# Scoring order of a token pass: the narrowest block's steps among a wide block's, another block at the end, and the passes without a loop

## The reference, cut to what matters

```python
x = x + _L0_conv_ref(_gn(x), L0_conv_W)                # sums of |w - patch|
x = _L1_conv_ref(x, ...)                               # two quantised 3x3 convolutions
t = _to_tokens(x)                                      # 16 images, 784 tokens, 128 channels
t = t + _L2_attn_ref(_ln_t(t), L2_attn_W, L2_attn_v)
t = t + _L2_ffn_ref(_ln_t(t), ...)                     # top 2 of 8 experts
t = t + _L3_attn_ref(_ln_t(t), ...)                    # causal linear attention
t = t + _L3_ffn_ref(_ln_t(t), ...)                     # spectral filters, plus 3 taps

def _L2_attn_ref(B, W, v):
    Wi = jnp.einsum('bnd,ed->bne', B, W)
    scores = jnp.einsum('d,bijd->bij', v, jnp.tanh(Wi[:, None, :, :] + Wi[:, :, None, :]))
    attn = jax.nn.softmax(scores, axis=-1)
    return jnp.einsum('bij,bjd->bid', attn, B)
```

## Time and profile before

| | |
|---|---|
| median of 3 runs (lowest, highest) | 12419.64 us (12418.51, 12423.34) |
| the profiled execution | 12419.25 us, span 12417.5 us |
| granted TensorE clock, mean of the span | 0.982 |
| first scoring matmul of pass 0; start of pass 2; last corner matmul | 6201.7, 6879.2, 12071.8 us |

### The profile page before, as it was taken

The page is one execution under the profiler, slowest core; times in us unless marked ns, Lnnn a source line. Parts: engine busy times, 40 slices in busy tenths (PEclk is TensorE's granted clock), DMA queues, the critical chain, the costliest instruction groups (busy, mean ns, idle before and its releaser), DMA issues. The chain is left out here.

```text
span 12417.5 us, 297675 instructions
## 1 busy us (share of the span) xinstructions
PE 11680.7 (94%) x123040; PEld 5800.0 (47%) x123040; DVE 11221.2 (90%) x20963; ACT 10972.2 (88%) x8020; POOL 125.0 (1%) x103
## 2 busy tenths in 40 slices
PE   8999999999999999999867999999999999999999
PEld 3333333333333333333323555555555555555567
DVE  9999999999999999999898888898888888888881
ACT  8999999999999999999788888888888888888872
POOL 0000000000000000000000000000000000000000
PEclk9999999999999999999988999999999999999999
DMA  0000000000000000000010111111111111111123
GB/s 14 2 7 2 3 6 2 7 2 4 4 2 7 2 4 4 2 4 2 16 51 3 45 53 53 53 54 50 50 53 53 54 54 50 52 51 55 51 57 109
DMA packets 290050, 355.16 MB, mean 29 GB/s; under 512 B 28040, under 2 KB 242960, under 8 KB 288656
## 3 DMA queue, kind: packets, MB, share of 16 engines
q1 hardware_dynamic: 288656, 335.48, 9.3%
HBM read 314.14 MB, written 21.23 MB: 27 GB/s over the span
## 5 line engine op out<-in xcount | busy, mean ns | idle before, releaser
L276 ACT ACTIVATE c_ring<-c_xn,c_w_neg 128x1568 f32<-128x1568 f32 x3824 | 5792.1, 1606 | 279.6 <-PE c_acc L235 273.0
L235 PE MATMUL c_acc<-c_ring,c_onehot 128*32 128x392 f32 x68608 | 5763.0, 493 | 138.5 <-DVE c_ring L434 78.8
L426 DVE TENSOR_SCALAR c_ring<-c_xn,c_w 128x1568 f32<-128x1568 f32 x4752 | 4572.9, 1036 | 93.2 <-PE c_acc L235 93.1
L1429 DVE TENSOR_SCALAR t_ring<-t_proj 128x172 f32<-128x172 f32 (+8 forms) x9664 | 3738.2, 462 | 361.4 <-PE t_psS L1010 330.7
L235 PEld LDWEIGHTS c_acc<-c_ring,c_onehot 128*32 128x32 f32 x68608 | 2217.4, 110 | 3658.0 <-issue 3209.2
L1110 ACT ACTIVATE t_ring<-t_ring 128x2624 f32<-128x2624 f32 (+63 forms) x1584 | 3306.5, 2118 | 502.8 <-DVE t_ring L1429 452.8
L1010 PE MATMUL t_psS<-t_ring,t_vhot 128*32 128x272 f32 (+22 forms) x36864 | 2369.8, 406 | 379.6 <-ACT t_ring L1109 165.9
L1010 PEld LDWEIGHTS t_psS<-t_ring,t_vhot 128*32 128x32 f32 x36864 | 1026.7, 113 | 1597.1 <-issue 918.9
L967 PE MATMUL t_psC<-t_filter_work 128*128 128x392 f32 (+3 forms) x6144 | 1654.4, 405 | 0.0
L967 PEld LDWEIGHTS t_psC<-t_filter_work 128*128 128x128 f32 x6144 | 1098.8, 190 | 688.0 <-issue 173.8
L434 DVE SCALAR_TENSOR_TENSOR c_ring<-c_xn,c_w,c_ring 128x784 f32<-128x784 f32 x1280 | 1267.6, 1034 | 95.8 <-ACT c_ring L276 94.8
(11 more groups left out here) (233 smaller groups left out, 3504.0 us busy)
## 6 DMA issues: line engine op xcount, KB each, us to landing
t_filter_work<-in_toep_dram SPq DMA_DIRECT2D x256, 393.0 KB, 3.4
t_filter_work<-mix_scratch SPq DMA_DIRECT2D x512, 192.0 KB, 2.5
t_filter_work<-in_toep_dram SPq DMA_DIRECT2D x256, 197.0 KB, 3.0
t_filter_work<-mix_scratch SPq DMA_DIRECT2D x512, 64.0 KB, 1.9
mix_scratch<-t_filter_work SPq DMA_DIRECT2D x4, 2048.0 KB, 9.5
c_xin<-in_x_dram SPq DMA_DIRECT2D x8, 784.0 KB, 4.3
x_scratch<-c_x1o SPq DMA_DIRECT2D x8, 784.0 KB, 3.4
t_proj<-x_scratch SPq DMA_DIRECT2D x16, 392.0 KB, 3.9
```

The source lines that it names most:

```text
L235: mm = pe.matmul(acc[32 * g:32 * g + 32, ch, 0:HALF], onehot[:, 31 - r:63 - r], ring[:, s % RING, g, ch * HALF:(ch + 1) * HALF], start=(s ...
L276: ins = act.activation(tile4(ring[:, s % RING, g, :]), window(xn, tap), ACT.Relu, bias=w0_neg[:, tap, 4 * r + g:4 * r + g + 1])
L426: dve.tensor_scalar(tile4(ring[:, s % RING, g, :]), window(xn, tap), w0[:, tap, 4 * r + g:4 * r + g + 1], 0.0, ALU.subtract, ALU.max).then ...
L1429: ins = dve.tensor_scalar(ring[:, st % RINGS, o + q * w:o + (q + 1) * w], proj[:, 128 * blk + first:T], proj[:, i:i + 1], None, ALU.add)
```

## The change

Block 5's steps are put among block 1's: one after every fourth, seven in all, and the corner after the last. Blocks then go 0, 4, 1 (with 5 and the corner), 2, 3, and block 3, two rows a step, ends the pass; its scores are copied out in the next. Batches follow the ends of blocks: after slot 86 (block 1's last) a batch comes one slot early and every fourth from there. Convolutions leave out batch 16; the last four mixes go together into batch 33, after the last slot. Side work past slot 86 moves by one slot or one batch, the next image's by one batch. Block 5's and the corner's matmuls no longer carry the flag that starts a sum, since block 1's first matmul has set their half bank. SyncE loads the next image when ScalarE, not VectorE, has ended the pass before. All passes are written out. No instruction that computes is added or taken away.

```diff
-ORDER = [0, 4, 1, 3, 2, 5, 6]
+ORDER = [0, 4, 1, 5, 6, 2, 3]
...
-START = {blk: sum(STEPS[o] for o in ORDER[:POS[blk]]) for blk in ORDER}
-NS = START[6]
+SLOTS = []
+for _blk in (0, 4, 1, 2, 3):
+    for _k in range(STEPS[_blk]):
+        SLOTS.append((_blk, _k))
+        if _blk == 1 and _k % 4 == 3 and _k // 4 < STEPS[5]: SLOTS.append((5, _k // 4))
+NS = len(SLOTS)
+END = {blk: 1 + max(st for st, slot in enumerate(SLOTS) if slot[0] == blk) for blk in STEPS}
...
-SLOTS = [(blk, k) for blk in ORDER[:6] for k in range(STEPS[blk])]
-assert len(SLOTS) == NS and NS % RINGS == 0
+assert sorted(SLOTS) == [(blk, k) for blk in range(6) for k in range(STEPS[blk])] and NS % RINGS == 0
...
-BATCHES = {min(GROUP * B + GROUP - 1, NS - 1) for B in range((NS + GROUP - 1) // GROUP)}
+BATCH_AT = [4 * B + 3 if 4 * B + 3 < END[1] else 4 * B + 2 for B in range((NS + GROUP - 1) // GROUP)]
+assert BATCH_AT[-1] == NS - 1 and all(END[blk] - 1 in BATCH_AT for blk in range(5))
 def batch(B, rank):
-    return min(GROUP * B + GROUP - 1, NS - 1) + rank
+    return BATCH_AT[B] + rank
+def filters_in(j):
+    return j if j < 16 else j + 1
...
+AT_LN = [dict(stats=28, aggr=30, norm=32, turn=batch(8, EARLY), evac=35), dict(stats=80, aggr=82, norm=84, turn=batch(21, EARLY), evac=86),
+         dict(stats=119, aggr=120, norm=122, turn=batch(31, EARLY), evac=126)]
...
-AT_STU = dict(u=batch(32, EARLY), uev=131, res=batch(3, LATE), resev=16, conv=[batch(u // 2, (FIRST, SECOND)[u % 2]) for u in range(64)], conved=[4 * (u // 2) + (3, 5)[u % 2] for u in range(64)],
-              mix=[batch(1 + m // 2, MIX) for m in range(64)], ar=[batch(1, EARLY), batch(17, EARLY)], out=[68, 1])
...
+AT_STU = dict(u=batch(32, EARLY), uev=130, res=batch(3, LATE), resev=16, conv=[batch(filters_in(u // 2), (FIRST, SECOND)[u % 2]) for u in range(64)],
+              conved=[int(batch(filters_in(u // 2), (0, 2)[u % 2])) for u in range(64)],
+              mix=[batch(1 + filters_in(min(m // 2, 29)) if m // 2 < 30 else 33, MIX) for m in range(64)], ar=[batch(1, EARLY), batch(17, EARLY)], out=[68, 1])
+AT_NEXT = dict(x=[batch(25, EARLY), batch(25, LATE)], tok=[102, 103], ln=dict(stats=104, aggr=106, norm=108), t=[batch(28, EARLY), batch(28, LATE)], tev=[114, 115],
+               w=[batch(29, EARLY), batch(29, LATE)], wev=[118, 119])
...
-            for b in range(3): one_pass(b, b % 2)
-            trips = (NI - 4) // 2
-            with e.Fori(0, trips) as bb:
-                one_pass(2 * bb + 3, 1, bb)
-                one_pass(2 * bb + 4, 0, bb)
-            one_pass(NI - 1, 1)
+            for b in range(NI): one_pass(b, b % 2)
...
-                W(sp, sums, 1, b - 1)
+                W(sp, th, 1, b - 1)
...
-                        if k == 0: W(pe, Sev, 0 if pos == 0 else scored(pos - 1), b)
+                        if k == 0 and blk < 5: W(pe, Sev, 0 if pos == 0 else scored(pos - 1), b)
...
-                                                    start=(r == 0), stop=(r == 31), skip_group_check=True)
+                                                    start=(r == 0 and blk != 5), stop=(r == 31), skip_group_check=True)
                         ins.then_inc(s_credit, 1)
-                        if st in BATCHES: step(st + 0.99)
-                    W(pe, cth, 1, b)
...
-                    ins.then_inc(pK.s, 1)
+                        if (blk, k) == (5, STEPS[5] - 1):
+                            W(pe, cth, 1, b)
+                            for r in range(TAIL):
+                                ins = pe.matmul(psS[0:32, CORNER_AT:CORNER_AT + TAIL], vhot[:, 31 - r:63 - r], corner[:, TAIL * r:TAIL * (r + 1)], start=False, stop=(r == TAIL - 1), skip_group_check=True)
+                            ins.then_inc(pK.s, 1)
+                        if st in BATCH_AT: step(st + 0.99)
...
+                        if (blk, k) == (5, STEPS[5] - 1):
+                            W(act, csum, 1, b)
+                            act.activation(corner[:, :], corner[:, :], ACT.Tanh).then_inc(cth.s, 1)
                         step(st - LEAD_ACT)
-                    W(act, csum, 1, b)
-                    act.activation(corner[:, :], corner[:, :], ACT.Tanh).then_inc(cth.s, 1)
...
-                if blk < 5: dve.wait_ge(s_credit, NS * b + START[blk] + STEPS[blk])
+                if blk < 5: dve.wait_ge(s_credit, NS * b + END[blk])
...
-                for blk in ORDER[:5]:
-                    yield START[blk] + STEPS[blk] + AT_EVAC
+                for blk in ORDER[:-1]:
+                    yield END[min(blk, 1) if blk > 4 else blk] + AT_EVAC
                     evac(blk, b)
...
             def last_evacs(d):
                 yield -1
-                evac(5, d); evac(6, d)
+                evac(ORDER[-1], d)
             def filled(name, blk, b, lo, hi):
                 dve.wait_ge(s_fmade, use(name, b))
```

More of the change, by code:

```diff
@@ L547 @@
 AT_NEW = {0: dict(fill=[batch(9, EARLY), batch(9, LATE)], filled=[39, 40], rowmax=41, diag=41, m=batch(10, EARLY), sub=43, exp=44, out=batch(11, EARLY), add=47),
-          1: dict(fill=[batch(20, LATE), batch(21, EARLY)], filled=[84, 87], rowmax=88, diag=88, m=batch(22, EARLY), sub=91, exp=92, out=batch(23, EARLY), add=95)}
-AT_LN = [dict(stats=28, aggr=30, norm=32, turn=batch(8, EARLY), evac=35), dict(stats=80, aggr=82, norm=84, turn=batch(21, EARLY), evac=87),
-         dict(stats=120, aggr=121, norm=123, turn=batch(31, EARLY), evac=127)]
+          1: dict(fill=[batch(21, LATE), batch(22, EARLY)], filled=[87, 90], rowmax=91, diag=91, m=batch(23, EARLY), sub=94, exp=95, out=batch(24, EARLY), add=98)}
@@ L556 @@
[L556 to L559 removed]
+AT_LIN = dict(q=batch(22, EARLY), zq=90, eq=91, qout=92, k=batch(23, EARLY), zk=94, ek=95, kout=96, v=batch(24, EARLY), vout=98,
+              a=[batch(24, LATE), batch(25, EARLY), batch(25, LATE), batch(26, EARLY), batch(26, EARLY), batch(26, LATE), batch(26, LATE)], apart=[99, 102, 103, 106, 106, 107, 107],
+              n=[batch(27, LATE), batch(27, LATE), batch(28, EARLY), batch(28, EARLY), batch(28, LATE), batch(28, LATE), batch(29, EARLY)], npart=[111, 111, 114, 114, 115, 115, 118])
@@ L1010, in body @@
                                     ins = pe.matmul(psS[32 * q:32 * q + 32, at + lo:at + hi], vhot[:, 31 - r:63 - r], ring[:, st % RINGS, c + lo:c + hi],
-                                                    start=(r == 0), stop=(r == 31), skip_group_check=True)
+                                                    start=(r == 0 and blk != 5), stop=(r == 31), skip_group_check=True)
                         ins.then_inc(s_credit, 1)
-                        if st in BATCHES: step(st + 0.99)
-                    W(pe, cth, 1, b)
-                    for r in range(TAIL):
-                        ins = pe.matmul(psS[0:32, CORNER_AT:CORNER_AT + TAIL], vhot[:, 31 - r:63 - r], corner[:, TAIL * r:TAIL * (r + 1)], start=(r == 0), stop=(r == TAIL - 1), skip_group_check=True)
-                    ins.then_inc(pK.s, 1)
+                        if (blk, k) == (5, STEPS[5] - 1):
[4 more added lines that the diff above has]
+                        if st in BATCH_AT: step(st + 0.99)
                 run(tracks, body)
@@ L1435, in body @@
                                               proj[:, i:i + R].unsqueeze(2).to_broadcast([128, R, w]), ALU.add).then_inc(sums.s, 1)
+                        if (blk, k) == (5, STEPS[5] - 1):
+                            pj = proj[:, T - TAIL:T]
+                            dve.tensor_tensor(corner[:, :].rearrange("p (a b) -> p a b", a=TAIL), pj.unsqueeze(1).to_broadcast([128, TAIL, TAIL]), pj.unsqueeze(2).to_broadcast([128, TAIL, TAIL]), ALU.add).then_inc(csum.s, 1)
                         step(st - LEAD_DVE)
-                    pj = proj[:, T - TAIL:T]
-                    dve.tensor_tensor(corner[:, :].rearrange("p (a b) -> p a b", a=TAIL), pj.unsqueeze(1).to_broadcast([128, TAIL, TAIL]), pj.unsqueeze(2).to_broadcast([128, TAIL, TAIL]), ALU.add).then_inc(csum.s, 1)
                 due = [next(track, None) for track in tracks]
```

5 lines of the change are left out of this document (removed).

## The result

| | before | after |
|---|---|---|
| median (lowest, highest) | 12420.58 us (12418.51, 12423.34), 4 runs | 12335.38 us (12331.94, 12337.03), 4 runs |
| profiled execution, span | 12419.25, 12417.5 | 12331.94, 12330.2 |
| steady passes 3 to 14, mean | 372.0 | 365.1 |

The ratio is 0.9931, its 95% interval 0.9914 to 0.9948: faster by 85 us, more than the 25 us that a measurement can tell. The forecast was 12417 and no change. The time lies in the range of 12300 to 12480, but outside the 12370 to 12455 in which the forecast itself was to stand; it is nearer to the first rival's 12285 (50 us) than to the forecast (82 us).

The account below looks back on a forecast made before the run. TensorE was taken to set the pass length, with 20.8 us idle; 13.6 removed and 3.3 plus 10.3 added left 20.8. With 4 us off passes 0 and 1 and 2 us more in the last: 12417 us, range 12300 to 12480.

Parts of the forecast that it names:

- the first rival: Steady passes: the 13.6 us are gained, queued work covers the new places but for 3.6; 12285 us, chance 0.24.
- passes written out: Loop of passes: 2 us for each of five turns between bodies, 10 us, counted in TensorE's waits.
- block 5 and corner into block 1: End of pass to slots 64 to 86: 8.4 us of TensorE waits removed a pass, 3.3 idle added.
- block 3 to the end: End of pass: 10.3 us of TensorE idle added, 5.2 of tanh waits removed a pass; last pass 2 us longer.
- ScalarE's chain: Slot 120 to block 0's fourth step: ScalarE works 54.3 us without a break, leaving TensorE idle 10.3.
- the old end: End of pass with block 5 and the corner: TensorE waits of 2.3, 1.6 and 4.5 us, 8.4 together, removed.
- The ledger as a whole: TensorE's idle time in a steady pass: 20.8 us less 13.6, plus 3.3 and 10.3, is 20.8 again.
- Two microseconds a turn: Loop's turns: each costs 2 us, from VectorE's 13.1 us of issue gaps and pass 8 (373.2) against pass 3 (371.2).
- The middle: Slots 64 to 86: VectorE has 57.8 us of work, TensorE 51.4; 3.3 counted as TensorE idle up to block 2.
- The small waits: Steady pass: 7.2 us of TensorE waits kept, the small ones, the linear attention's and 1.2 at block 4.
- all alike: Sign that the forecast is right: steady passes of 371 to 372 us, without differences between them.
- VectorE becomes the bound in block 1: Slots 64 to 90: TensorE idles 9.9 us there, 6.6 more a pass; 12503 us, chance 0.13.

Follow-up runs that it names:

- the written-out kernel: The kernel before with all sixteen passes written out and nothing else changed: 12396.69 us, ratio 0.998.
- block 2 last: The changed kernel with block 3 back between blocks 1 and 2, so that block 2 ends the pass: 12329.23 us, ratio 0.9926.
- the run with five more tanhs: The changed kernel with five more unread tanhs a pass on ScalarE in block 3: 12358.47 us; the same five in block 2 instead: 12335.34 us.
- the fitted fillers: The changed kernel with unread matmuls fitted into three TensorE waits (6, 7 and 5): 12325.55 us, ratio 0.9924.
- the long ones: The changed kernel with 11, 12 and 9 unread matmuls in the same three TensorE waits: 12330.03 us, ratio 0.9926.
- the two kernels with the moved normalisation: Second normalisation one slot earlier, copies of blocks 1, 5 and corner too: in the changed kernel 12355.2 us, in the one with block 2 last 12354.24 us.
- the kernel with block 2 last and fillers: The kernel whose passes end in block 2, with 9, 3, 8 and 5 unread matmuls in TensorE's waits: 12321.33 us, ratio 0.9921.
- fitted fillers in both: Besides the changed kernel so filled, the kernel before, written out, with 8, 7 and 14 unread matmuls in its three end-of-pass waits: 12384.92 us, ratio 0.997.
- the filled kernel: The kernel before, loop kept, with 12, 10 and 20 unread matmuls in three TensorE waits at the end of a pass: 12442.32 us, ratio 1.0018.

## Why the prediction was right and wrong

The measured time is in the range, but the account behind the forecast is not borne out: that no change would come rested on a sum of which the largest added term, 68 us, came to 6. The range held because it was wide enough to take in half of the first rival. Its three parts against the runs, for the whole program:

| part | forecast | measured, by |
|---|---|---|
| passes written out | -10 us | -24.5, the written-out kernel |
| block 5 and corner into block 1 | -60 (7.6 removed, which is the 8.4 less what the turns hold of it, 3.3 added, 13 passes; 4 in the first two) | -67.5, from there to block 2 last |
| block 3 to the end | +68 (10.3 added, 5.2 removed, 13 passes; 2 at the last) | +6, from there to after |

**The step that failed is the last one,** "ScalarE's chain": not its length but what it was set against. From the end of slot 118 to the end of block 0's fourth step I had 56.7 us; the mean is 56.5. That ScalarE works through it without a break is what 55.57 of 55.90 us and the run with five more tanhs show (1.5 us more in this stretch). Idle time was to be 10.3; it is 8.1, and 2.7 of half-clock excess fill the rest. But the forecast booked all 10.3 as added to an end of pass that costs nothing, once block 5 and the corner are gone from it. With block 2 last TensorE still waits 2.6 us from slot 134 to slot 3 and 1.4 before slot 134: block 0's tanhs, 18.8 us for seven, come late whatever block stands before them. The forecast named what goes with the old end (8.4) and did not ask what is late next. And block 3's old place was priced at its waits alone, 5.2; with block 2 last it is 6.3 idle and 3.6 at half clock. Taken together (idle and excess, from slot 86's end to slot 3's, cut at slot 118's end in both kernels): block 3's move brings the first stretch from 11.1 to 4.5 and the second from 4.3 to 10.8, 6.6 less and 6.5 more. The runs show this balance; that it is as even as this is a matter of these two arrangements and was not to be expected from the terms.

**The ledger as a whole** held only idle time: 20.8, less 13.6, plus 13.6. By the traces it is 21.3 idle and 5.4 of excess before, 17.1 and 2.7 after. But the excess is no sum of its own to be subtracted either. With fillers most or all of it vanished in four kernels: 4.8 us a pass bought 1.2, 3.0 bought 0.7, 2.7 bought 0.6 with the fitted fillers and 0.1 with the long ones, which overran their waits. Taken away by fillers, then, a quarter of it or less comes back; the waits that follow grow by the rest. But passes of one kernel set side by side can show it nearly whole: 3.1 of 3.2 us and 1.6 of 1.7 in block 2 of the two kernels with the moved normalisation, 1.6 of 1.7 a pass in the kernel with block 2 last and fillers. I read the two together so, which no run shows alone: what an amount of it costs depends on whether a wait stands behind it that takes it up. The Trainium skill (TensorE: Matmul & The Clock Gate, HAM oscillation — how this bites in real kernels) prices throttled time at half its length, all of it as added time, which for a busy TensorE is this excess. The three cases side by side agree with that; of what the fillers took away a quarter or less had been added. The clock has little part in the 85 us: with fitted fillers in both, the changed kernel is 59 us under the written-out one (12325.55 and 12384.92), without them 61.

**Written out.** Two microseconds a turn was read from VectorE's issue gaps and from one pair of passes. A turn also stops TensorE, for some 6.9 us as the filled kernel showed, under cover of the copies, and lengthens the pass behind it too: passes with a turn took 373.3 us, those after them 370.9, and written out the mean is 369.8. The comparison of pass 8 with pass 3 could not show the second, since pass 3's own 371.2 us are 369.4 when written out. In the changed kernel the same turn costs 1.6, under the forecast's 2.

**Right.** The middle: from slot 64's first matmul to slot 87's it takes 54.5 us, 50.8 of them busy, where 51.4 and 3.3 idle were told (the parts given for batches 20 and 21 add up to 17.4, not 16.7, which changes little). TensorE's idle time from slot 63 to block 2 is 0.8, 1.25 and 1.5, 3.5 us. Two of the three stand where they were told, before the transposes of the second normalisation and for block 1's copies; but it is block 2's first transposes that wait for these, not its first step. No issue gap on VectorE, no wait for copied scores at a pass's start, the next image's load hidden. The small waits stayed but for the linear attention's, 1.0 and not 2.2 a pass (13.3 us for L1388 against 28.6 for L1377). The tail stayed: 347.5 us from the last scoring matmul on, four mixes among them, against 345.7. Wrong besides: "all alike" (the clock's three-pass order), and passes 0 to 2: pass 3 starts 15 us earlier by block 5's move and 8 later by block 3's, where a gain of 4 was forecast for the first and nothing for the second.

**The rivals.** "The gain comes through" had the right sign and 10 us a pass; 6.9 came. Its picture, queued work that covers the new places, is not what happened either: TensorE idles 8.1 us at the new end. "VectorE becomes the bound in block 1" did not happen: its busy time there is 51.10 us of 53.30. Its mechanism exists all the same, as the moved normalisation showed by 20 us.

What stays open: why the same wait of 3.08 us lowers the clock in one pass and not in another, and how a turn's stop is covered in the changed kernel.

## What to carry to other kernels

Before a new arrangement is charged with its waits, work out the same stretch for the arrangement that it replaces, with the work that remains: the wait that comes next is part of the price of both. An engine's idle time that is taken away is worth what the next slowest engine leaves of it, and a cheap way to see this is to give that engine a few instructions more, once in each place: two microseconds a pass cost 23 us in one and nothing in the other. An operation that copies something for a waiting engine stands in a queue; moving other work ahead of it moves the wait, and one long wait can be dearer than two short ones of nearly the same sum, when the clock falls behind it.

## What the hardware showed that I had not expected

- Turning a loop of two passes cost 4.9 us in one kernel and 1.6 in the other. TensorE stood for 4.38 and then 2.53 us behind the branch with nothing that the profile shows to wait for, while VectorE's gap was 2.43.
- The granted clock fell behind some waits of 2.1 to 3.1 us and not behind others of the same length at the same place: 12 matmuls took 1.77 and 3.30 us behind 3.08 us of idling.
- Such falls made the lengths of passes with the same instructions repeat in threes, 369.1, 362.0 and 364.6; with the waits filled they were 365.0 each.
- Work at half clock cost nearly its whole excess between passes of one kernel (1.6 of 1.7 us, 3.1 of 3.2), but filling the waits before it gave back a quarter or less (1.2 of 4.8, 0.7 of 3.0, 0.6 of 2.7).
- Matmuls that nobody reads, put into waits that are longer than they, made three kernels faster, by 8 to 12 us in 12400. Where they filled the waits to the end the gain was 5 us or none, and behind the loop's turn they cost 21.
